# Four gathers of a batch's expert results on GpSimd: one in each of four slots, in place of all four in one slot

## The chip, the cores and the metric

The kernel runs on one core of a Trainium2 chip. Times are device microseconds of one execution of the whole program on that core. The engines are TensorE (PE, with its weight loads as PEld), VectorE (DVE), ScalarE (ACT), GpSimd (POOL) and SyncE (SP, which only issues transfers here).

## The reference, cut to what matters

Eight batches of 256 tokens with 128 features go through a layer norm, and from it through two branches that are added to the input: attention with 16 heads, a linear position bias and two learned null keys, and a mixture of experts (a shared expert, and the two best of eight experts for each token).

```
xn = layernorm(x)
q, k = l2norm(norm(xn) @ Wq) * q_scale, l2norm([null_k, xn @ Wkv_k]) * k_scale
attn = softmax(8 * q @ k.T + slope_h * bias, causal) @ [null_v, xn @ Wkv_v] @ Wout
w = top-2 of sigmoid(xn @ router), normalised
routed = sum over the token's 2 experts e of w_e * (silu(xn @ wg_e) * (xn @ wu_e)) @ wd_e
out = x + attn + shared(xn) + routed
```

## The kernel before, in words

The program has three stages. First the weights are turned and split into a high and a low part, the tokens are routed, and GpSimd scatters each token's row to two places of a DRAM tensor that is sorted by expert (`xg_dram`). Then 39 tiles of 128 rows go through their expert's matrices and are written to `yg_dram`. Last, from about 165 us of the span on, comes the attention stage, with which everything here has to do.

The attention stage works on one batch after the other. Each engine has its own instruction list, written by a function `entry(part, b)`: batch 0 is the part "first", batches 1 to 6 are one loop body "mid", batch 7 is "last", and a short "drain" follows. Each batch has 16 slots `s`, one for each head, and the work on one head is spread over slots by a lag: head `h` has its scores in slot `h` (PE L1072, DVE L885, which adds the bias and finds the maximum), its exponential in slot `h + 1` (ACT L649), its division by the sum in slot `h + 2` (DVE L869), its transposes in slot `h + 3` (PE L1063), and so on. A slot number that a lag drives past 15 falls into the next batch. In a table, `JOBS`, side jobs are laid down slot by slot: the projections of the next batch ("kq", "v"), the transposes of queries and keys ("tr"), the shared expert ("sh") and the final sum of the batch before ("yt"). PE does a side job in its slot, the other engines handle it one slot later. All engines run their lists in order and meet only by semaphores.

GpSimd's list in a batch is this. In slots 0 and 1 it splits the next batch's tokens into a high and a low part (L446, L449; PE's "kq" job of slot 1 waits for the first pair), in slot 2 the same for the current batch (L466, L469). One slot after each "kq" job it raises eight sums of squares to the power -0.5 (`norms`, L415 or L418 and L421; it waits for DVE's L850) and multiplies 512 columns by them (`scale_by_norm`, L431). PE's "kq" jobs stand in slots 1, 4, 5, 6, 7, 11, 12 and 13, so these norms stand in slots 2, 5, 6, 7, 8, 12, 13 and 14. In each odd slot it copies two heads' probabilities of the null keys (L484, `pnull`) after it has waited for DVE's L869 (semaphore `pn`); ACT's L649 may overwrite a ring place of `prob` only after that copy (semaphore `pnc`). In slots 7 and 10 it splits half of the shared expert's hidden values (L457, L459). In slot 10, last, it waits for `fin` (the final sum of the batch before has read `yg` and `w_now`), copies the batch's row numbers and weights (`slot_now` L489, `w_now` L490), waits for these copies, and issues four indirect DMAs (L495) that gather the batch's expert results from `yg_dram` into `yg`: 2 token tiles by 2 experts, 128 rows of 512 bytes each. DVE reads `yg` in the "yt" job, in slot 8 of the next batch (L839).

Of the kernel before, what the change touches and what calls it, by code (L numbers as in the profile page):

```python
# [19 lines left out]
E, I, TOPK = 8, 256, 2  # L20
NT = BATCH * SEQ // P
TB = SEQ // P
# [17 lines left out]
def build(nc, a, out):  # L40


    with ExitStack() as ctx:
        def sb(name, shape, dt=F32):
            return ctx.enter_context(nc.sbuf_tensor(name, shape, dt))
# [8 lines left out]
        yg_dram = nc.dram_tensor("slot_y", [SLOTS, DIM], F32).ap()  # L54
# [34 lines left out]
        def carve(n):  # L89
            at[0] += n  # L90
            return arena_b[:, at[0] - n:at[0]]
# [24 lines left out]
        yg = carve(TB * TOPK * DIM).rearrange("p (t c d) -> p t c d", c=TOPK, d=DIM)  # L116
# [27 lines left out]
        slot_now = sb("slot_now", [P, TB, TOPK], I32)  # L144
# [59 lines left out]
        g = type("Sems", (), S)  # L204
# [48 lines left out]
        def count(part, i, until=HEADS):  # L253

            return sum(1 for job in part_jobs(part, i) if job[0] < until)

        def behind(part, b, s, lag):


            if s < lag:  # L260
                part, b, s = {"mid": "mid", "last": "mid", "drain": "last"}.get(part), b - 1, s + HEADS
            return [(part, b, job) for job in jobs(part, b, s - lag)] if part else []
# [25 lines left out]
        def head_at(part, s, lag):  # L288

            h = s - lag  # L290
            return h if (("own" if h >= 0 else "prev") in PARTS[part]) else None
# [16 lines left out]
        def settled(eng):  # L308


            eng.sem_inc(g.passed, 1)
# [48 lines left out]
        def _(pool):  # L360
# [47 lines left out]
            def norms(b, job):  # L408
                kind, c, w, t, i, n = job
                if kind == "kq":  # L410
                    j = nth(c, w, t)
                    nb = b + 1
                    pool.wait_ge(g.ssm_ready, 8 * nb + j + 1)
                    if w == 0:
                        gp.tensor_tensor(rnorm[:, j, :], ssm[:, j, :], mhalf[:, 0:HEADS // 2],  # L415
                                         ALU.pow).then_inc(g.r_ready, 1)
                    else:
                        gp.tensor_tensor(rpow[:, j, :], ssm[:, j, :], mhalf[:, 0:HEADS // 2],  # L418
                                         ALU.pow).then_inc(g.pw, 1)
                        pool.wait_ge(g.pw, 4 * nb + 2 * c + t + 1)  # L420
                        gp.tensor_tensor(rnorm[:, j, :], rpow[:, j, :], rslope[:, c * 8:c * 8 + 8],  # L421
                                         ALU.mult).then_inc(g.r_ready, 1)

            def scale_by_norm(b, job):
                kind, c, w, t, i, n = job
                if kind == "kq":
                    j = nth(c, w, t)
                    pool.wait_ge(g.r_ready, 8 * (b + 1) + j + 1)
                    pool.wait_ge(left[i], n + 1)
                    rows = (qtok if w else ktok)[t][:, c * 512:(c + 1) * 512].rearrange("p (h d) -> p h d", d=DH)  # L430
                    gp.tensor_tensor(rows, rows, bc(rnorm[:, j, :], DH), ALU.mult).then_inc(g.kqn, 1)  # L431

            def entry(part, b, steps=range(HEADS)):
                whose = PARTS[part]
                nb = b + 1
                for s in steps:
                    if s < 2 and "next" in whose and part != "ready":
                        xT, xs = ((xn2T, xs2), (xn1T, xs1))[s]
                        for _, _, (kind, c, w, t, i, n) in (x for lag in range(1, HEADS) for x in behind(part, b, s, lag)):
                            if (kind, c, w, t) == (("kq", 1, 1, 1), ("v", 0, 0, 1))[s]:  # L440
                                pool.wait_ge(filled[i], n + 1)
                        if part == "first":
                            for i in range(2):
                                pool.wait_ge(filled[i], count("ahead", i) + count("ready", i))
                        settled(pool)
                        gp.tensor_copy(xs[0], xT[:, bass.ds(nb * SEQ, SEQ)]).then_inc(g.xhi, 1)  # L446
                        pool.wait_ge(g.xhi, 2 * nb + s + 1)
                        settled(pool)
                        gp.tensor_tensor(xs[1], xT[:, bass.ds(nb * SEQ, SEQ)], xs[0].bitcast(F32),  # L449
                                         ALU.subtract).then_inc(g.xlo, 1)  # L450
                    if s in (7, 10) and "own" in whose:
                        c = (7, 10).index(s)
                        pool.wait_ge(g.sh_h, 2 * b + c + 1)
                        if part != "first":
                            pool.wait_ge(g.shd, b)
                        settled(pool)
                        gp.tensor_copy(hss[0][:, c * SEQ:(c + 1) * SEQ], hs[:, c, :]).then_inc(g.sh_hi, 1)  # L457
                        pool.wait_ge(g.sh_hi, 2 * b + c + 1)
                        gp.tensor_tensor(hss[1][:, c * SEQ:(c + 1) * SEQ], hs[:, c, :],  # L459
                                         hss[0][:, c * SEQ:(c + 1) * SEQ].bitcast(F32), ALU.subtract).then_inc(g.sh_lo, 1)  # L460
                    if s == 2 and "own" in whose:
                        for _, _, (kind, c, _, t, i, n) in (x for lag in range(1, HEADS) for x in behind(part, b, s, lag)):
                            if (kind, c) == ("sh", 1):
                                pool.wait_ge(filled[i], n + 1)
                        settled(pool)
                        gp.tensor_copy(xs_late[0][:], xn1T[:, bass.ds(b * SEQ, SEQ)]).then_inc(g.late_hi, 1)  # L466
                        pool.wait_ge(g.late_hi, b + 1)
                        settled(pool)
                        gp.tensor_tensor(xs_late[1][:], xn1T[:, bass.ds(b * SEQ, SEQ)], xs_late[0][:].bitcast(F32),  # L469
                                         ALU.subtract).then_inc(g.late_lo, 1)  # L470
                    h = head_at(part, s, 2)
                    for _, job_b, job in (behind(part, b, s, 1) if part != "ahead" else []):
                        norms(job_b, job)
                        scale_by_norm(job_b, job)
                    if h is not None and h % 2:
                        p = h // 2
                        pool.wait_ge(g.pn, TB * (HEADS * b + h + 1))
                        if p == 0 and part != "first":
                            pool.wait_ge(g.pn_hi, 2 * b)
                        settled(pool)  # L480
                        q = p % PAIRS
                        two = prob[:, h % 4 - 1:h % 4 + 1, :]
                        for t, c0 in ((0, 0), (1, K0)):
                            gp.tensor_copy(pnull[:, t, 4 * q:4 * q + 4].rearrange("p (h n) -> p h n", n=2),  # L484
                                           two[:, :, c0:c0 + NNULL]).then_inc(g.pnc, 1)
                    if s == 10 and "own" in whose:
                        pool.wait_ge(g.fin, b + 1)
                        settled(pool)
                        gp.tensor_copy(slot_now[:], slot[:, bass.ds(b * TB, TB), :]).then_inc(g.now, 1)  # L489
                        gp.tensor_copy(w_now[:], wts[:, bass.ds(b * TB, TB), :]).then_inc(g.now, 1)  # L490
                        pool.wait_ge(g.now, 2 * b + 2)
                        settled(pool)
                        for t in range(TB):
                            for c in range(TOPK):
                                pool.indirect_dma_start(yg[:, t, c, :], None, yg_dram,  # L495
                                                        bass.IndirectOffsetOnAxis(ap=slot_now[:, t, c:c + 1], axis=0)
                                                        ).then_inc(g.gath, 16)

            for n in range(NT * TOPK):
                if n == 15:  # L500
                    pool.wait_ge(g.t_ev, 8)
                if n in (15, 22):
                    entry("ahead", -1, [n // 22])
                scatter(n)
# [7 lines left out]
            with pool.Fori(1, BATCH - 1) as b:  # L512
                entry("mid", b)
# [663 lines left out]
```

## Time and profile before

| what | value |
|---|---|
| median of 3 runs | 530.21 us (529.77 to 532.17) |
| the profiled execution | 529.1 us, of which its span 527.4 us |
| mean granted clock of PE in it, share of full speed | 0.96 |
| PE busy, share of the span | 425.0 us, 81% |
| DVE busy | 405.1 us, 77% |
| ACT busy | 358.5 us, 68% |
| POOL busy | 328.2 us, 62% |
| from one batch's first gather to the next one's in the loop | 45.90 us |

The span is the time between the first and the last event that the profiler recorded; 1.7 us of the execution lie around it. Busy times of PE are modelled from its pipelined matmuls, so they are an upper view.

### The profile page before, as it was taken

Reading aid. Unit: us, or ns where it says so; the run is one execution under the profiler, and the core shown is the slowest. Engines: PE = TensorE matmul, PEld = TensorE weight load, DVE = VectorE, ACT = ScalarE, POOL = GpSimd, SP = SyncE. Lnnn points to the kernel's source line nnn. Section 1 sums busy time; section 2 is a strip of 40 time slices with the busy share of each in tenths; the row PEclk is TensorE's granted clock in tenths of the full one; section 3 lists DMA queues with packets and bytes.
Section 4 is the critical chain, followed back from the end, with each engine's and each line's share of the span. In section 5 each row is a group of like instructions: output and inputs, shape, how many; then the busy total and the mean of one; then the engine's idle time right before and its main releaser. Section 6 shows DMA issues by size and latency. Waiting matters only on the chain.

```text
span 527.4 us, 11888 instructions
## 1 busy us (share of the span) xinstructions
PE 425.0 (81%) x2857; PEld 310.8 (59%) x2857; DVE 405.1 (77%) x1466; ACT 358.5 (68%) x1092; POOL 328.2 (62%) x492
## 2 busy tenths in 40 slices
PE   0657243999997889979988996998899699899885
PEld 0555121677775667657656764765676476567663
DVE  3854713666652899888988988998898899889885
ACT  1334123566666878968886895888689688768864
POOL 2275778940002789678867957876795887777140
PEclk9999767899999999989998999999899999989999
DMA  7940111222221000000001000000100000010010
GB/s 219 350 134 32 45 45 59 56 75 79 78 68 32 1 12 11 2 21 22 0 0 30 10 0 20 20 0 0 34 6 0 20 20 0 0 35 5 2 42 10
DMA packets 28159, 21.04 MB, mean 40 GB/s; under 512 B 3512, under 2 KB 25312, under 8 KB 28000
## 3 DMA queue, kind: packets, MB, share of 16 engines
q1 hardware_dynamic: 25264, 16.46, 10.5%
q0 software_dynamic: 2048, 4.20, 2.7%
q8 instruction: 13, 0.21, 0.2%
q14 instruction: 18, 0.15, 0.1%
q10 hardware_dynamic: 816, 0.03, 0.1%
HBM read 12.41 MB, written 8.26 MB: 39 GB/s over the span
## 4 chain that ended last, share of the span: by engine, by line
POOL 31%; PE 21%; issue 20%; DVE 15%; DMA 5%; ACT 4%; POOLq 1%; SPq 1%; DVEq 1%; ACTq 0%
POOL rnorm L415 6%; POOL slot_x L405 6%; POOL arena_b L495 6%; POOL rpow L418 5%; PE bank L1140 4%; PE bank L930 3%; DVE arena_b L885 3%; DVE arena_b L869 3%; POOL pnull L484 3%; PE bank L932 3%; PE bank L931 3%; DMA arena_b<-in_L_ffn_wu_dram 2%; DMA arena_b<-slot_x 2%; PE bank L1072 2%; DVE ssq L846 2%
## 5 line engine op out<-in xcount | busy, mean ns | idle before, releaser
L649 ACT ACTIVATE arena_b<-arena_b,nmx 128x130 f32<-128x130 f32 (+1 forms) x256 | 115.2, 458 | 29.5 <-DVE nmx L885 20.5
L869 DVE TENSOR_SCALAR arena_b<-arena_b,rden 128x130 f32<-128x130 f32 (+1 forms) x256 | 103.9, 450 | 4.5
L885 DVE CUSTOM_DVE_ANT_0 arena_b<-bank,bias 128x130 f32<-128x130 f32 (+1 forms) x256 | 80.9, 353 | 17.1 <-PE bank L1072 9.3
L1072 PE MATMUL bank<-arena_a 64*128 64x130 f32 (+1 forms) x512 | 59.8, 352 | 23.6 <-DVE nmx L885 22.8
L418 POOL TENSOR_TENSOR rpow<-ssm,mhalf 128x8 f32<-128x8 f32 x32 | 52.7, 1648 | 40.4 <-DVE ssm L850 40.4
L1063 PE MATMUL bank<-ident,arena_b 128*128 128x128 f32 x384 | 67.2, 284 | 7.1 <-DVE arena_b L869 7.1
L431 POOL TENSOR_TENSOR arena_b<-arena_b,rnorm 128x512 f32<-128x512 f32 x64 | 67.1, 1048 | 8.4 <-POOL rnorm L421 3.8
L587 ACT ACTIVATE arena_b<-bank 128x512 f32<-128x512 f32 x64 | 38.2, 597 | 31.3 <-PE bank L932 30.5
L415 POOL TENSOR_TENSOR rnorm<-ssm,mhalf 128x8 f32<-128x8 f32 x32 | 52.4, 1639 | 7.7 <-DVE ssm L850 7.7
L846 DVE TENSOR_REDUCE ssq<-arena_b 128x8 f32<-128x512 f32 x64 | 43.4, 678 | 15.5 <-ACT arena_b L587 15.2
L1072 PEld LDWEIGHTS bank<-arena_a 64*128 64x128 f32 x512 | 33.6, 186 | 36.4 <-DVE nmx L885 30.4
L1063 PEld LDWEIGHTS bank<-ident,arena_b 128*128 128x128 f32 x384 | 42.1, 141 | 20.5 <-DVE arena_b L869 12.1
L649 ACT ACTIVATION_READ_ACCUMULATOR arena_b<-arena_b,nmx 128x1 f32 x256 | 50.8, 198 | 0.0
L877 DVE COPY probT<-bank 128x384 f32<-128x384 f32 x64 | 35.5, 555 | 11.1 <-PE bank L1063 7.0
L1053 PE MATMUL bank<-probT,arena_a 128*64 128x256 f32 x256 | 43.1, 410 | 0.8 <-DVE arena_r L860 0.8
L1018 PE MATMUL bank<-ident,arena_b 128*128 128x128 f32 x256 | 39.5, 278 | 4.4 <-ACT arena_a L596 2.8
L405 POOL DMA_INDIRECT slot_x<-arena_a,slot x32 | 32.7, 1022 | 15.6 <-issue 9.2
L495 POOL DMA_INDIRECT arena_b<-slot_y,slot_now x32 | 32.1, 1003 | 13.8 <-issue 7.3
L1018 PEld LDWEIGHTS bank<-ident,arena_b 128*128 128x128 f32 x256 | 29.3, 140 | 16.1 <-issue 9.4
L588 ACT ACTIVATE arena_b<-bank 128x512 f32<-128x512 f32 x64 | 38.1, 596 | 0.0
L446 POOL CAST arena_r<-xn2T 128x256 fp32r (+1 forms) x8 | 3.2, 394 | 54.7 <-PE bank L932 54.7
L484 POOL COPY pnull<-arena_b 128x4 f32<-128x4 f32 x128 | 24.4, 219 | 18.7 <-DVE arena_b L869 18.7
(209 smaller groups left out, 1111.7 us busy)
## 6 DMA issues: line engine op xcount, KB each, us to landing
slot_x<-probT SPq DMA_DIRECT2D x3, 832.0 KB, 9.8
arena_b<-slot_x SPq DMA_DIRECT2D x39, 64.0 KB, 1.9
slot_y<-arena_b SPq DMA_DIRECT2D x39, 64.0 KB, 1.5
arena_b<-in_L_ffn_wd_dram SPq DMA_DIRECT2D x1, 1024.0 KB, 9.4
arena_b<-in_L_attn_Wkv_dram SPq DMA_DIRECT2D x1, 1024.0 KB, 8.6
arena_b<-in_L_attn_x_dram SPq DMA_DIRECT2D x8, 128.0 KB, 2.1
out_dram<-arena_b SPq DMA_DIRECT2D x8, 128.0 KB, 1.8
arena_b<-in_L_attn_Wq_dram SPq DMA_DIRECT2D x1, 512.0 KB, 6.5
```

What stands on the lines that cost most here:

```text
L405: pool.indirect_dma_start(xg_dram, bass.IndirectOffsetOnAxis(ap=slot[:, n // TOPK, n % TOPK:n % TOPK + 1], axis=0), xn1[:, n // TOPK, :], ...
L415: gp.tensor_tensor(rnorm[:, j, :], ssm[:, j, :], mhalf[:, 0:HEADS // 2], ALU.pow).then_inc(g.r_ready, 1)
L418: gp.tensor_tensor(rpow[:, j, :], ssm[:, j, :], mhalf[:, 0:HEADS // 2], ALU.pow).then_inc(g.pw, 1)
L431: gp.tensor_tensor(rows, rows, bc(rnorm[:, j, :], DH), ALU.mult).then_inc(g.kqn, 1)
L495: pool.indirect_dma_start(yg[:, t, c, :], None, yg_dram, bass.IndirectOffsetOnAxis(ap=slot_now[:, t, c:c + 1], axis=0)).then_inc(g.gath, 16)
L649: sc.activation(prob[:, h % 4, c], sim[h % 2][:, c], ACT.Exp, scale=-1.0, bias=nmx[:, h % HEADS, t:t + 1], accum_out=den[:, h % HEADS, t:t ...
L846: ve.reduce_sum(ssq[j % 2][:], sqb[j % 2].rearrange("p (h d) -> p h d", d=DH), AX.X).then_inc(g.red, 1)
L869: ve.tensor_scalar(pr, pr, rden[:, h % HEADS, t:t + 1], None, ALU.mult).then_inc(g.pn, 1)
L885: ve.tensor_tensor_reduce(out=sim[h % 2][:, c], in0=bank[h % 2][:, c], in1=bias[:, c], scale=-SLOPES[h], scalar=3e38, op0=ALU.add, op1=ALU ...
L1018: ins = te.transpose(side[i][:, q * P:(q + 1) * P], src[:, p * P:(p + 1) * P], ident[:])
L1063: ins = te.transpose(bank[2 + h % 2][:, k * P:(k + 1) * P], prob[:, h % 4, c:c + P], ident[:])
L1072: ins = te.matmul(bank[half][:, c0:c1], qT[r, h // 2, q0:q0 + P], kT[r, h // 2, 0:c1 - c0], start=True, stop=True)
```

## The change

The condition around the four issues is moved. In place of all four in slot 10, behind the copy of the row numbers, gather 0 stays in slot 10, and gathers 1, 2 and 3 come last in GpSimd's slots 11, 12 and 13. Their order, their operands and what they signal are the same, and no wait is added or taken away.

```
                         gp.tensor_copy(w_now[:], wts[:, bass.ds(b * TB, TB), :]).then_inc(g.now, 1)
                         pool.wait_ge(g.now, 2 * b + 2)
                         settled(pool)
-                        for t in range(TB):
-                            for c in range(TOPK):
-                                pool.indirect_dma_start(yg[:, t, c, :], None, yg_dram,
-                                                        bass.IndirectOffsetOnAxis(ap=slot_now[:, t, c:c + 1], axis=0)
-                                                        ).then_inc(g.gath, 16)
+                    if 10 <= s < 10 + TB * TOPK and "own" in whose:
+                        t, c = (s - 10) // TOPK, (s - 10) % TOPK
+                        pool.indirect_dma_start(yg[:, t, c, :], None, yg_dram,
+                                                bass.IndirectOffsetOnAxis(ap=slot_now[:, t, c:c + 1], axis=0)
+                                                ).then_inc(g.gath, 16)
```

## Rows read from the trace of the kernel before

**Rows 1.** The page's busy time: engine, us, share of the span.

```profile
PE 425.0 (81%) x2857; PEld 310.8 (59%) x2857; DVE 405.1 (77%) x1466; ACT 358.5 (68%) x1092; POOL 328.2 (62%) x492
```

**Rows 2.** Waits in 215 to 495 us: us in total, times, longest.

```profile
POOL rpow L418 <- DVE ssm L850: 36.4, 18, 3.4
...
ACT arena_b L649 <- POOL pnull L484: 5.3, 6, 0.9
...
PEld bank L930 <- POOL arena_r L449: 3.6, 5, 0.7
...
PE bank L930 <- POOL arena_r L449: 2.4, 5, 0.5
```

**Rows 3.** Busy time of the engines from 376 to 398 us.

```profile
376.00:398.00 22.00, 21.52 (x168) 15.67 (x164) 20.15 (x77) 19.11 (x60) 18.13 (x29) 1.00 0.05 12
```

**Rows 4.** POOL in order of time, a batch of the loop: start, us.

```profile
371.97 1.64 POOL L418 TENSOR_TENSOR rpow<-ssm,mhalf 128x8 f32<-128x8 f32 x1 [1.58 <-DVE ssm L850]
...
377.68 1.08 POOL L495 DMA_INDIRECT arena_b<-slot_y,slot_now  x1 [0.80 <-POOL w_now L490]
379.06 0.95 POOL L495 DMA_INDIRECT arena_b<-slot_y,slot_now  x1 [0.30 <-issue]
380.32 1.05 POOL L495 DMA_INDIRECT arena_b<-slot_y,slot_now  x1 [0.30 <-issue]
381.68 0.94 POOL L495 DMA_INDIRECT arena_b<-slot_y,slot_now  x1 [0.30 <-issue]
382.63 0.42 POOL L484 COPY pnull<-arena_b 128x4 f32<-128x4 f32 x2
383.02 1.67 POOL L418 TENSOR_TENSOR rpow<-ssm,mhalf 128x8 f32<-128x8 f32 x1
...
392.41 0.39 POOL L446 CAST arena_r<-xn2T 128x256 fp32r x1
392.99 0.72 POOL L449 TENSOR_TENSOR arena_r<-xn2T,arena_r 128x256 fp32r<-128x256 f32 x1 [0.19 <-POOL arena_r L446]
```

**Rows 5.** DVE in order of time, the same batch.

```profile
371.72 0.17 DVE L850 TENSOR_SCALAR ssm<-ssq 128x8 f32<-128x8 f32 x1
...
377.50 0.55 DVE L869 TENSOR_SCALAR arena_b<-arena_b,rden 128x130 f32<-128x130 f32 x2
...
380.00 0.56 DVE L869 TENSOR_SCALAR arena_b<-arena_b,rden 128x130 f32<-128x130 f32 x2
...
381.28 0.17 DVE L850 TENSOR_SCALAR ssm<-ssq 128x8 f32<-128x8 f32 x1
...
385.40 1.12 DVE L869 TENSOR_SCALAR arena_b<-arena_b,rden 128x130 f32<-128x130 f32 x2
...
391.22 1.20 DVE L869 TENSOR_SCALAR arena_b<-arena_b,rden 128x130 f32<-128x130 f32 x2
```

**Rows 6.** PE in order of time, the next batch's slots 1 to 3.

```profile
393.77 0.50 PE L930 MATMUL bank<-wq_hi,arena_r 128*128 128x512 f32 x1 [0.48 <-POOL arena_r L449]
...
400.84 0.93 PE L1072 MATMUL bank<-arena_a 64*128 64x130 f32 x8 [0.35 <-DVE nmx L885]
```

**Rows 7.** POOL in order of time: a scatter behind a tensor instruction.

```profile
65.72 1.00 POOL L405 DMA_INDIRECT slot_x<-arena_a,slot  x1 [0.16 <-issue]
```

**Rows 8.** POOL, then DVE, in batch 0: the same places.

```profile
199.42 1.67 POOL L418 TENSOR_TENSOR rpow<-ssm,mhalf 128x8 f32<-128x8 f32 x1
...
197.44 0.17 DVE L850 TENSOR_SCALAR ssm<-ssq 128x8 f32<-128x8 f32 x1
```

**Rows 9.** ACT, the exponential of slot 13 in batch 7.

```profile
512.11 0.41 ACT L649 ACTIVATE arena_b<-arena_b,nmx 128x130 f32<-128x130 f32 x1 [1.72 <-POOL pnull L484]
```

**Rows 10.** The line L495: from issue to landing.

```profile
DMA to landing us min/median/max: 2.4/2.6/3.5
```

## The prediction

> **What bounds the kernel now.** I first read the page's busy times [rows 1]. No engine is full, so the shares alone decide nothing: PE has 81%, DVE 77%, POOL 62%. In the attention stage a batch takes 45.90 us, and the four gathers stand where three engines are dense together: from 376 to 398 us PE is busy for 21.5 of 22 us, DVE for 20.2 and POOL for 18.1 [rows 3]. Next the waits of the loop [rows 2]. POOL waits 36.4 us in total for DVE's L850, but always in the first half of a batch; in the second half others wait for POOL: PE's "kq" matmul of slot 1 for the split L449 (PEld up to 0.7 us, five times), and ACT's exponential for the copy L484 (0.9 us, six times). So POOL's list from slot 10 to slot 0 of the next batch is on the path that sets a batch's length, and it is enough to follow it in order of time [rows 4]. After the fourth gather POOL doesn't wait once for another engine until slot 0: it is behind, and works off its list. From the end of gather 0 at 378.76 to the first split of the next batch at 392.41 it takes 13.65 us. The split L449 then ends at 393.71 and PE starts on it at 393.77, after 0.48 us of idle [rows 6].
>
> **What the change removes, adds and moves.** No instruction is added or removed. On POOL, gathers 1, 2 and 3 move behind the copy L484 of slot 11, behind the norms of slot 12, and behind norms and copy of slot 13. What is still behind the last of them is slot 14's norms, slot 15's copy, and slot 0.
>
> Slot 11: the copy needs head 9's L869, which ends at 378.05 [rows 5], before gather 0 ends at 378.76. So it runs at once (0.42 us) and stands 3.87 us earlier than now. Gather 1 follows. The price of a gather after a tensor instruction isn't shown, but a scatter behind one is: 0.16 us of gap and 1.00 us [rows 7]. So gather 1 ends at 378.76 + 0.42 + 1.16 = 380.34.
>
> Slot 12: here a wait appears. The power L418 needs DVE's L850, which ends at 381.28 + 0.17 = 381.45 [rows 5]. In slot 8 the power started 0.08 us after that instruction's end (371.89 to 371.97) [rows 4, 5]. So it starts at 381.53, and POOL has been idle for 1.2 us, where now it isn't idle at all. DVE can't be earlier: nothing of the change reaches it before then, and PE and DVE are both nearly full there [rows 3]. The power starts 383.02 - 381.53 = 1.49 us earlier than now.
>
> Slots 12 to 15: the norms and copies take what they take now (9.39 us from 383.02 to 392.41), and gathers 2 and 3 come on top, 2 x 1.16 = 2.32 us. Both later sums of squares are ready in time, since POOL reaches them at most 0.4 us earlier than now, or later. So slot 0 begins 2.32 - 1.49 = 0.83 us later than now. In batch 0 the same sum is 199.42 - (197.44 + 0.17 + 0.08) = 1.73 us gained [rows 8], and 2.32 - 1.73 = 0.59 us lost. The gain that one might expect, that the norms come sooner, is real only for slots 11 and 12, and nobody waits for these.
>
> Both ends of the gather's price: with no gap and the shortest duration it is 0.94 us, and the shift 1.88 - 1.49 = 0.39 us. With the gap of the first gather now (0.80 us, of which part is a wait for its row numbers) and 1.08 us, it is 1.88, and the shift 3.76 - 1.49 = 2.27 us. I take 1.16, since rows 7 is the one row with a tensor instruction in front. The gaps of 0.30 between gathers now are behind another gather [rows 4].
>
> How much of 0.83 us reaches the end of the batch: PE starts the "kq" of slot 1 0.83 us later, and does the rest of slots 1 to 3 behind it. But in slot 3 it waits 0.35 us for DVE in any case [rows 6], so only what exceeds 0.35 goes on: 0.48 us a batch. Behind that point the stage is a chain of waits between PE, ACT and DVE, and I know of no cover. Slot 0's splits stand in batches 1 to 6 only. So the loss is 0.24 (behind batch 0) + 5 x 0.48 = 2.6 us.
>
> The end gains: batch 7 has no splits in slot 0 and no norms in slots 12 to 14, so there only the copies count. Behind batch 6, ACT's wait of 0.9 us [rows 2] shrinks, because the copy of slot 13 comes 1.49 - 1.16 = 0.33 us earlier: -0.3 us. In batch 7 ACT waits 1.72 us for the copy behind four gathers [rows 9]; this copy now stands behind one. DVE's scores are ready about 0.8 us before 512.11, so no more than that can be won, and I take 0.5 us, since DVE has further waits behind it.
>
> Sum: 2.6 - 0.3 - 0.5 = +1.8 us. The landing is no term: a gather lands 2.6 us after its issue [rows 10], and DVE reads `yg` only in slot 8 of the next batch, in batch 7 at the very end, after more than 10 us. The other side of POOL's order is free too: `fin` is waited for as before, ahead of gather 0.
>
> **A rule on the shared port.** Now gathers that start during DVE's L869 (377.68 and 380.32) take 1.08 and 1.05 us, the others 0.95 [rows 4, 5]: 0.1 us more. The Trainium skill ("SBUF — State Buffer", Who interferes with whom, and the warning on descriptors in SBUF: two separate sides) says that a DVE instruction in a two-port mode holds the port pair that it shares with GpSimd for its whole length, so that GpSimd can't write descriptors. By this rule gather 2, which will stand across slot 14's L869, would be held for all of it. By the trace it is 0.1 us.
>
> **The rivals.**
> 1. *The whole shift goes through* (slower): PE's 0.35 us is no cover, for example because ACT's line behind the "kq" (its square, two copies, the exponential) is itself without a gap. Then the loss is 0.59 + 5 x 0.83 = 4.7 us, less 0.8: +3.9 us, 534.1. For it speaks that ACT has its own work behind that matmul.
> 2. *DVE sets the pace and becomes faster* (faster). DVE's L869 takes 0.55 us beside a gather or a power, and 1.12 and 1.20 us in slots 14 and 0, where it runs beside L431 [rows 4, 5]. With the new order a gather stands beside slot 14's and a power beside slot 0's, which gives up to 0.57 + 0.65 = 1.2 us a batch. It decides only if slot 0 on POOL isn't later than now, that is if the gathers cost no more than 0.75 us each there. Then PE could win its idle of 0.48 us [rows 6] in six batches, 2.9 us, and the end 0.8: -3.7 us, 526.5. Against it: no gather in the trace takes less than 0.94.
> 3. *A gather is held by DVE* for a whole L869 (0.55 us in place of 0.1), one gather a batch: 6 x 0.45 = 2.7 us on top of the sum, 534.7. Against it stand the 1.05 to 1.08 us of now. This is what the page's rule would make of it.
> 4. *Each separate gather pays the first one's gap*: shift 2.27 us, in batch 0 3.76 - 1.73 = 2.03, so 5 x 1.92 + 1.68 - 0.8 = +10.5 us, 540.7.
>
> **How the numbers follow.** By its own time the profiled execution goes from 529.1 to 530.9 us (span 527.4 to 529.2). The median before is 530.21, 1.1 above the profiled execution, and I put the 1.8 us on it: 532.0. Chances: this forecast 0.45, rival 1 0.25, rival 2 0.1, rival 3 0.08, rival 4 0.05, something else 0.07. The range reaches from the lower end of the gather's price, 529.6 (no loss behind batch 0 to 5, and the end's gain), rounded out a little to 529.0, up to 535.5, past rivals 1 and 3; rivals 2 and 4 are left out. A measurement can tell about 0.5%, 2.65 us, from no change, that is 527.6 to 532.9. Of the forecast's 0.45, 0.38 lies inside this; rivals 1, 3 and 4 lie above it, rival 2 below it but for a part. That makes faster 0.1, same 0.48, slower 0.42.
>
> **What would show it right or wrong.** In POOL's line of the changed kernel: L484 of slot 11 directly behind gather 0; a wait of 1.0 to 1.3 us for DVE's L850 before slot 12's L418, seven times, where there is none now; gathers with gaps near 0.16 us; L446 of slot 0 some 14.5 us after the end of gather 0 in place of 13.65. PE's wait for L449 grows from 0.5 to about 1.3 us; ACT's waits for L484 shrink, the one of 1.72 us is gone. The distance of two batches' first gathers goes from 45.90 to about 46.4 us. L869 in slots 14 and 0 is back at 0.55 us. The prediction is wrong if DVE delivers slot 12's sum sooner than now (then POOL doesn't wait), if a separate gather costs clearly more or less than 1.16 us, or if slots 1 to 3 swallow all or nothing of the shift.

## The result and the profile after

The changed kernel takes **538.14 us** (median of six runs, 536.07 to 542.12), the kernel before beside it 529.99 us (six runs, 528.74 to 532.17). The ratio is 1.0166, with a 95% interval of 1.0118 to 1.0214: slower by 8.2 us. Forecast were 532.0 us and a range of 529.0 to 535.5. The sign of the sum was right, its size was not. The profiled execution is the slowest of the six, 542.12 us with a span of 540.4 us, so the spans of the two profiles differ by 13.0 us, more than the medians do.

The waits between 215 and 495 us of the changed kernel, in the order of [rows 2] (us in total, times, longest):

```profile
POOL rpow L418 <- DVE ssm L850: 44.2, 20, 4.8
...
PEld bank L930 <- POOL arena_r L449: 9.8, 5, 2.0
PE bank L930 <- POOL arena_r L449: 8.6, 5, 1.8
...
ACT arena_b L649 <- POOL pnull L484: 6.1, 6, 1.1
```

GpSimd's list over one batch of the loop and into the next, the lines that answer to [rows 4]:

```profile
338.26 1.07 POOL L495 DMA_INDIRECT arena_b<-slot_y,slot_now  x1 [0.80 <-POOL w_now L490]
339.35 0.32 POOL L484 COPY pnull<-arena_b 128x4 f32<-128x4 f32 x2
339.82 0.97 POOL L495 DMA_INDIRECT arena_b<-slot_y,slot_now  x1 [0.15 <-issue]
342.11 1.68 POOL L418 TENSOR_TENSOR rpow<-ssm,mhalf 128x8 f32<-128x8 f32 x1 [1.32 <-DVE ssm L850]
...
344.22 1.04 POOL L431 TENSOR_TENSOR arena_b<-arena_b,rnorm 128x512 f32<-128x512 f32 x1 [0.16 <-POOL rnorm L421]
345.43 1.05 POOL L495 DMA_INDIRECT arena_b<-slot_y,slot_now  x1 [0.16 <-issue]
346.51 1.68 POOL L415 TENSOR_TENSOR rnorm<-ssm,mhalf 128x8 f32<-128x8 f32 x1
...
349.87 1.06 POOL L495 DMA_INDIRECT arena_b<-slot_y,slot_now  x1 [0.16 <-issue]
...
354.18 0.39 POOL L446 CAST arena_r<-xn2T 128x256 fp32r x1
```

The reader is to see four things. The copy of slot 11 stands directly behind gather 0. Slot 12's power waits 1.32 us for DVE's sum, where it waited for nothing. It starts 2.78 us after the end of gather 0 (339.33 to 342.11); the forecast had 2.77. And from the end of gather 0 to the first split L446 it is now 14.85 us, where it was 13.65 and 14.5 were forecast. Up to the power the forecast holds to 0.01 us, so the rest lies behind it, in the two gathers there. From the start of slot 12's power to the first split it was 9.39 us (383.02 to 392.41), and it is now 12.07 us (342.11 to 354.18) with two gathers in it. So a separate gather costs 2.68 / 2 = 1.34 us of the list and not 1.16. Its 0.16 us of gap is right. But it takes 1.05 us and not 1.00 (the median of the 32 is 1.052 us, and before it was 0.952), and 0.13 us more go where it meets the next instruction. The kernel before shows the same place without a gather:

```profile
385.13 1.04 POOL L431 TENSOR_TENSOR arena_b<-arena_b,rnorm 128x512 f32<-128x512 f32 x1 [0.16 <-POOL rnorm L421]
386.13 1.64 POOL L415 TENSOR_TENSOR rnorm<-ssm,mhalf 128x8 f32<-128x8 f32 x1
```

There the power starts 0.04 us before the recorded end of L431 and takes 1.64 us. Behind a gather it starts 0.03 us after the gather's end and takes 1.68.

PE, in two neighbouring batches, from the wait for L449 on (to be laid beside [rows 6]):

```profile
355.54 0.56 PE L930 MATMUL bank<-wq_hi,arena_r 128*128 128x512 f32 x1 [1.70 <-POOL arena_r L449]
355.89 0.63 PE L931 MATMUL bank<-wq_hi,arena_r 128*128 128x512 f32 x1
356.32 0.63 PE L932 MATMUL bank<-wq_lo,arena_r 128*128 128x512 f32 x1
356.74 1.06 PE L1018 MATMUL bank<-ident,arena_b 128*128 128x128 f32 x4
...
404.12 0.50 PE L930 MATMUL bank<-wq_hi,arena_r 128*128 128x512 f32 x1 [1.69 <-POOL arena_r L449]
404.45 0.39 PE L931 MATMUL bank<-wq_hi,arena_r 128*128 128x512 f32 x1
404.68 0.39 PE L932 MATMUL bank<-wq_lo,arena_r 128*128 128x512 f32 x1
404.91 0.60 PE L1018 MATMUL bank<-ident,arena_b 128*128 128x128 f32 x4
```

The wait has grown from 0.48 to 1.7 us, as much as the shift of 1.20 us. What the prediction had not reckoned with stands behind it: in the one batch the same instructions take 0.63 and 1.06 us, in the other 0.39 and 0.60. The windows around the first of them (busy us of PE, PEld, DVE, ACT and POOL, then the granted clock of PE) give the reason:

```profile
353.00:355.00 2.00, 0.84 (x9) 0.43 (x5) 1.97 (x7) 0.95 (x4) 1.81 (x5) 1.00 0.00 0
355.00:357.00 2.00, 1.46 (x5) 1.11 (x6) 1.53 (x6) 0.61 (x3) 1.81 (x5) 0.71 0.00 0
357.00:359.00 2.00, 2.00 (x10) 1.68 (x8) 0.95 (x3) 1.58 (x3) 1.43 (x4) 0.50 0.00 0
359.00:361.00 2.00, 2.00 (x17) 1.42 (x18) 0.72 (x5) 1.86 (x7) 1.76 (x3) 0.93 0.00 0
```

Behind the wait the granted clock falls from 1.00 (2.4 GHz) to 0.50 (1.2 GHz). The shares missing in the three windows add up to 0.58 + 1.00 + 0.14 = 1.7 us of full clock, just where PE already is late. It happens in three of the loop's six batches: behind the waits that end at 260, 356 and 451 us, and not behind two equally long ones in between. The Trainium skill ("TensorE: Matmul & The Clock Gate", Part 1: The HAM clock gate) says that TensorE is granted 1.2 GHz or 2.4 GHz, by how busy it has lately been; the two levels are these, and a fall behind an idle stretch is what the rows show.

How the 13.0 us lie over the span, by the start of the copy to `w_now` in each batch (worked out from the timelines of both profiles):

| stretch | before, us | after, us | difference |
|---|---|---|---|
| start to batch 0 | 193.18 | 193.97 | +0.8 |
| batch 0 to 1 | 45.72 | 47.67 | +1.95 |
| batch 1 to 6, no fall in slot 1 (two) | 45.88, 45.89 | 46.68, 46.68 | +0.8 each |
| batch 1 to 6, fall in slot 1 (three) | 45.89, 45.89, 45.89 | 48.82, 48.57, 48.29 | +2.9, +2.7, +2.4 |
| batch 6 to 7 | 37.51 | 38.53 | +1.0 |
| batch 7 to the end | 21.50 | 21.17 | -0.3 |

So the shift costs 0.8 us an interval, and a fall of the clock in slot 1 about 2 us more (5.6 us over the three). The kernel before has such falls too, four of 1.7 us of full clock in its loop, but all of them 38 to 39 us behind the copy to `w_now`, in the middle of the next batch. The interval of 45.89 us that holds one at 369 us is as long as the ones without. What counts is where the clock falls.

Not all of the 13.0 us come from the change. In the profile of the changed kernel the clock also falls ahead of batch 0's gathers, where the two kernels' lists are still the same. The same window, before and then after:

```profile
190.00:192.00 2.00, 1.24 (x13) 1.00 (x13) 1.77 (x8) 1.26 (x5) 1.84 (x6) 1.00 0.02 4
```

```profile
190.00:192.00 2.00, 2.00 (x13) 1.41 (x11) 1.08 (x4) 1.32 (x5) 1.84 (x3) 0.50 0.00 0
```

Behind it DVE's sum for slot 12 comes late, and so does the rest of the batch. Eleven of the study's fourteen profiles have such a fall between 186 and 197 us, the kernel before on the second chip among them, and in all eleven this sum starts 5.6 to 6.3 us behind the copy to `w_now`. In the three without it (the kernel before here, and the two runs below that move gathers into the next batch's slot 3) it is 4.3 us. The first experiment below has this fall, but in its loop a list no longer than before, and its interval from batch 0 to 1 is 46.61 us: some 0.9 us of the 1.95 go with the fall.

### The profile page after: what moved, and what is told of

Read it like the earlier page. It is cut to its first block, busy times and chain, and to the rows that moved or that the text cites. A ratio compares the mean times of both kernels' runs of the same rounds, so it can differ in the third digit from the quotient of the medians.

```text
span 540.4 us, 11888 instructions
## 1 busy us (share of the span) xinstructions
PE 433.5 (80%) x2857; PEld 317.5 (59%) x2857; DVE 402.3 (74%) x1466; ACT 360.4 (67%) x1092; POOL 331.7 (61%) x492
## 4 chain that ended last, share of the span: by engine, by line
PE 30%; POOL 24%; issue 19%; DVE 14%; DMA 5%; ACT 5%; SPq 1%; POOLq 1%; DVEq 1%; ACTq 0%
POOL slot_x L405 6%; POOL rnorm L415 5%; PE bank L930 4%; POOL arena_b L495 4%; PE bank L932 4%; PE bank L931 3%; POOL rpow L418 3%; PE bank L1072 3%; PE bank L1140 3%; DVE arena_b L885 3%; DVE arena_b L869 3%; DMA arena_b<-slot_x 3%; PE bank L1063 2%; PE bank L1053 2%; POOL pnull L484 2%
## 5 line engine op out<-in xcount | busy, mean ns | idle before, releaser
L869 DVE TENSOR_SCALAR arena_b<-arena_b,rden 128x130 f32<-128x130 f32 (+1 forms) x256 | 97.3, 429 | 4.6
L1072 PE MATMUL bank<-arena_a 64*128 64x130 f32 (+1 forms) x512 | 62.8, 366 | 22.8 <-DVE nmx L885 22.0
L1063 PE MATMUL bank<-ident,arena_b 128*128 128x128 f32 x384 | 68.6, 289 | 6.4 <-DVE arena_b L869 6.4
L431 POOL TENSOR_TENSOR arena_b<-arena_b,rnorm 128x512 f32<-128x512 f32 x64 | 67.1, 1049 | 8.4 <-POOL rnorm L421 3.8
L1072 PEld LDWEIGHTS bank<-arena_a 64*128 64x128 f32 x512 | 35.6, 196 | 35.8 <-DVE nmx L885 29.3
L1063 PEld LDWEIGHTS bank<-ident,arena_b 128*128 128x128 f32 x384 | 43.2, 144 | 19.8 <-DVE arena_b L869 11.3
L877 DVE COPY probT<-bank 128x384 f32<-128x384 f32 x64 | 35.6, 556 | 13.2 <-PE bank L1063 9.5
L1018 PE MATMUL bank<-ident,arena_b 128*128 128x128 f32 x256 | 40.9, 285 | 3.7 <-ACT arena_a L596 2.2
L495 POOL DMA_INDIRECT arena_b<-slot_y,slot_now x32 | 33.1, 1033 | 11.3 <-POOL w_now L490 6.5
L1018 PEld LDWEIGHTS bank<-ident,arena_b 128*128 128x128 f32 x256 | 30.4, 144 | 15.9 <-issue 8.3
L446 POOL CAST arena_r<-xn2T 128x256 fp32r (+1 forms) x8 | 3.2, 395 | 55.9 <-PE bank L932 55.9
L484 POOL COPY pnull<-arena_b 128x4 f32<-128x4 f32 x128 | 24.6, 221 | 20.0 <-DVE arena_b L869 19.8
```

The costliest lines, as they stand in the source:

```text
L495: pool.indirect_dma_start(yg[:, t, c, :], None, yg_dram, bass.IndirectOffsetOnAxis(ap=slot_now[:, t, c:c + 1], axis=0)).then_inc(g.gath, 16)
L869: ve.tensor_scalar(pr, pr, rden[:, h % HEADS, t:t + 1], None, ALU.mult).then_inc(g.pn, 1)
L1018: ins = te.transpose(side[i][:, q * P:(q + 1) * P], src[:, p * P:(p + 1) * P], ident[:])
L1063: ins = te.transpose(bank[2 + h % 2][:, k * P:(k + 1) * P], prob[:, h % 4, c:c + P], ident[:])
L1072: ins = te.matmul(bank[half][:, c0:c1], qT[r, h // 2, q0:q0 + P], kT[r, h // 2, 0:c1 - c0], start=True, stop=True)
```

## The experiments

All ratios are to runs of the kernel before on the same chip. Two chips were used: on the first the kernel before took 530.03 us (median of 23), on the second 536.49 (17) and 536.07 (22). Where an experiment has added lines, the later line numbers are 1 to 3 higher (L498 is L495).

**The idle filled.** If the loss is the idle before slot 12's power and gathers behind it, then gathers that fill the idle must take it back.

```diff
-                    if 10 <= s < 10 + TB * TOPK and "own" in whose:
-                        t, c = (s - 10) // TOPK, (s - 10) % TOPK
+                    for n in ({10: (0,), 11: (1, 2), 13: (3,)}.get(s, ()) if "own" in whose else ()):
+                        t, c = n // TOPK, n % TOPK
```

> Gather 0 in slot 10, gathers 1 and 2 in slot 11, gather 3 in slot 13: the changed kernel with gather 2 one slot earlier. Theory A (GpSimd idles 1.31 us before slot 12's power, and the two gathers behind it push slot 0 later): gather 2 costs 1.29 us on GpSimd's line and fills that idle time, so slot 0's L446 comes 13.5 to 13.7 us after the end of gather 0, as before (13.65; changed kernel 14.85), PE waits about 0.5 us for L449 and not 1.7, and the time is that of the kernel before, 529 to 531 us. Rival B (each gather that stands alone costs something by itself, by its gap or by VectorE's port): two of the three lone places are left, and at least half of the loss stays, 534 us or more.

It took 529.75 us (527.06 to 530.64), ratio 0.9979 (0.9960 to 0.9999). GpSimd's list in order of time:

```profile
379.92 0.32 POOL L484 COPY pnull<-arena_b 128x4 f32<-128x4 f32 x2
380.40 0.97 POOL L495 DMA_INDIRECT arena_b<-slot_y,slot_now  x1 [0.15 <-issue]
381.67 0.94 POOL L495 DMA_INDIRECT arena_b<-slot_y,slot_now  x1 [0.30 <-issue]
382.70 1.67 POOL L418 TENSOR_TENSOR rpow<-ssm,mhalf 128x8 f32<-128x8 f32 x1
```

Only 0.08 us of idle are left before the power, the loop's intervals are 45.66 to 45.69 us, and PE waits 0.27 us. That refutes rival B of the expectation, which kept at least half of the loss. The second form has the dictionary `{10: (0,), 11: (1, 2, 3)}`, all three in slot 11:

> Gather 0 in slot 10, gathers 1, 2 and 3 in slot 11, behind the copy L484. Theory A: only the copy comes forward by 3.9 us; nothing idles before slot 12's power, slot 0 is where it was, and in batch 7 ScalarE's wait of 1.7 us goes: 529 to 530.5 us. Rival B: no loss either, since the gathers stand together. Rival D (the copy's earlier place is what harms): slower than before by more than 3 us.

529.04 us (527.85 to 530.67), ratio 0.9986 (0.9971 to 1.0001), intervals of 45.66 us, a wait of 0.25. The earlier copy does no harm, so rival D is refuted too. Both take the whole loss back, and in the first a gather by itself in slot 13 does no harm, since another one has filled the idle ahead of slot 12's power.

**The gathers where GpSimd has time.** If GpSimd's list from slot 10 to slot 0 sets the length of a batch, it must be worth something to take gathers out of it. Here a batch's gathers stand in slots 3 and 4 of the next batch, and batch 7's in its own slot 10.

```diff
+                    here = {10: (0, 1, 2, 3)} if part == "last" else {}
+                    if part in ("mid", "last"):
+                        here = {3: (0, 1), 4: (2, 3), **here}
+                    for n in here.get(s, ()):
+                        t, c = n // TOPK, n % TOPK
```

> Batches 0 to 6: the four gathers leave slots 10 to 13 and stand in slots 3 and 4 of the next batch, two in each, where GpSimd waits 3.4 us for VectorE's sum of slot 5; batch 7 has all four in slot 10. Theory A: GpSimd's list from slot 10 to slot 0 is about 5 us shorter, L449 is ready before PE asks for it, and PE's wait (0.5 us before the change, 1.7 after) is 0 in batches 1 to 6: 3 us faster than before, 526 to 528 us. It waits instead for VectorE's sums in slots 12 to 14. If the four gathers (5.2 us) overrun the 3.4 us of idle time and slot 5's power gets onto the path, the gain is lost: 530 us or more. Rival B expects no gain from an earlier L449: 530 us.

It took **522.82 us** (519.18 to 526.88), ratio 0.9872 (0.9833 to 0.9912), the first kernel of the study that is faster than before. Intervals are 44.26 us. GpSimd, in two places of a batch:

```profile
332.92 1.64 POOL L418 TENSOR_TENSOR rpow<-ssm,mhalf 128x8 f32<-128x8 f32 x1 [2.98 <-DVE ssm L853]
...
342.03 0.40 POOL L446 CAST arena_r<-xn2T 128x256 fp32r x1
...
351.49 1.08 POOL L498 DMA_INDIRECT arena_b<-slot_y,slot_now  x1 [0.16 <-issue]
352.87 0.95 POOL L498 DMA_INDIRECT arena_b<-slot_y,slot_now  x1 [0.30 <-issue]
354.13 0.94 POOL L498 DMA_INDIRECT arena_b<-slot_y,slot_now  x1 [0.30 <-issue]
355.38 0.94 POOL L498 DMA_INDIRECT arena_b<-slot_y,slot_now  x1 [0.30 <-issue]
356.35 1.68 POOL L418 TENSOR_TENSOR rpow<-ssm,mhalf 128x8 f32<-128x8 f32 x1
```

In slot 12 it now waits 2.98 us for DVE, so of the 4.9 us of gathers that left only 1.8 shorten the list (14.07 us from the copy to `w_now` to the split, before 15.84), and the batch by 1.6. PE waits for no split any more. The gain is larger than the 3 us expected, which counted PE's wait alone: five intervals are 1.6 us shorter each, and the one behind batch 0 by 1.8. In the chain that ended last the shares have turned over, first the kernel before, then this one:

```profile
POOL 31%; PE 21%; issue 20%; DVE 15%; DMA 5%; ACT 4%; POOLq 1%; SPq 1%; DVEq 1%; ACTq 0%
```

```profile
PE 47%; DVE 21%; issue 11%; POOL 7%; ACT 6%; DMA 5%; SPq 1%; DVEq 1%; ACTq 0%; POOLq 0%
```

On the second chip the same was tried by halves: gathers 0 and 1 in the own slot 11, 2 and 3 in slot 3 of the next batch (batch 7: slots 11, 12 and 13).

> Gathers 0 and 1 in slot 11, where GpSimd now waits 3.0 us for slot 12's sum, gathers 2 and 3 in slot 3 of the next batch, where it waits 3 us for slot 5's; batch 7 has them in slots 11, 11, 12 and 13. With all four in slots 3 and 4 (522.8 us) slot 5's power came 1.8 us late. Theory A: each pair (2.5 us) fits into idle time, nothing on GpSimd is late, and the time is that of the late gathers or up to 2 us below, 520 to 523.5 us. If pairs cost time by their number of places, it is between them and before: 525 us.

525.66 us (524.84 to 526.79), ratio 0.9820 (0.9794 to 0.9847), intervals of 44.78 us. The expected 520 to 523.5 us were missed. The ratio is better than the 0.9872 of all four moved, but the kernel before is 6 us slower on this chip. By the intervals, moving all four is the better order: 44.26 against 44.78 us.

**The clock alone.** If the falls in slot 1 cost time of their own, then the changed kernel must win when PE is kept busy during its wait. Ten useless matmuls of 128 columns (the profile shows each as two) go ahead of the "kq" matmul of slot 1 in batches 1 to 6; nothing else differs from the changed kernel.

```diff
+                if (kind, c, w, t) == ("kq", 0, 1, 0) and not isinstance(n, int):
+                    for k in range(10):
+                        te.matmul(side[i][:, 0:P], ident[:], ident[:], start=True, stop=True)
```

> The changed kernel, and in batches 1 to 6 PE does ten more matmuls of 128 columns on the identity into the side bank that its slot-1 job is going to overwrite, just before it waits for L449: work without use, about 1.4 us, inside the wait of 1.7 us. Theory C (a part of the loss is that PE's granted clock falls to 1.2 GHz behind this wait in four of six batches, which costs about 2 us each time): the granted clock stays at 1.00 in slot 1, all distances of first gathers are about 46.7 us, and the time is 533.5 to 536 us, 2 to 5 us below the changed kernel. If the clock there costs nothing, the time stays at 538 us or rises.

537.93 us (535.56 to 539.07, five runs), ratio 1.0141 (1.0117 to 1.0165). PE and the windows at the place shown above:

```profile
352.98 2.40 PE L1011 MATMUL bank<-ident 128*128 128x128 f32 x20
355.13 0.48 PE L930 MATMUL bank<-wq_hi,arena_r 128*128 128x512 f32 x1
355.45 0.39 PE L931 MATMUL bank<-wq_hi,arena_r 128*128 128x512 f32 x1
```

```profile
353.00:355.00 2.00, 2.00 (x21) 2.00 (x20) 1.57 (x8) 1.26 (x5) 1.81 (x6) 1.00 0.00 0
355.00:357.00 2.00, 2.00 (x17) 1.78 (x15) 1.53 (x5) 0.79 (x2) 1.63 (x6) 1.00 0.00 0
```

The falls in slot 1 are gone (the expectation speaks of four, the changed kernel's profile has three) and the loop's intervals are even, 46.96 to 46.98 us. But ten matmuls last 0.3 us longer than the wait. The profile's span is 4.0 us below that of the changed kernel, but the median doesn't stand apart from its 538.14 us, and the expected 533.5 to 536 us were missed. So it was repeated on the second chip with eight (`range(8)`), beside the changed kernel once more.

> The changed kernel as it is, once more, beside the other runs of this call: 535 to 540 us, a ratio of 1.010 to 1.020. Its distances of first gathers are either about 46.7 us, where the granted clock stays up in slot 1, or 48 to 49 us, where it falls.

540.05 us (538.84 to 541.48), ratio 1.0087 (1.0057 to 1.0117), below the 1.010 to 1.020 expected: the kernel before lost more on this chip than the changed one. Its intervals are 46.68 to 46.79 us without a fall in slot 1 and 48.30 and 48.56 with one.

> As the run with ten matmuls without use in PE's wait of slot 1 (2.15 us, 0.3 us longer than the wait), now with eight (1.72 us), which fit into it. Theory C (the fall of the clock behind the wait costs about 2 us each time): no fall in slot 1, all distances in the loop 46.6 to 46.8 us, and the time 1 to 4 us below the changed kernel of the same call. If the clock costs nothing, the two are the same.

536.36 us (533.50 to 542.32, twelve runs), ratio 1.0003 (0.9975 to 1.0032). Both were run once more in the last series:

> The changed kernel once more, beside the others of this call: 1.008 to 1.018 of the kernel before; some distances of first gathers at 46.7 us, those with a fall of the granted clock in slot 1 at 48 to 49 us.

540.30 us (537.49 to 543.37), ratio 1.0089 (1.0061 to 1.0117). Three intervals with a fall in slot 1 take 48.25 to 48.34 us. In all, the three profiles of the changed kernel have eighteen waits of 1.4 to 1.8 us there, and eight of them are followed by a fall.

> The changed kernel with eight matmuls without use in PE's wait of slot 1, once more. Theory C: 2 to 5 us below the changed kernel of this call, as in the last call (536.4 against 540.1 us), and no fall of the clock in slot 1.

536.54 us (533.89 to 539.05, twelve runs), ratio 1.0022 (1.0002 to 1.0042). PE in one place of its loop, and the window behind it:

```profile
350.28 1.95 PE L1011 MATMUL bank<-ident 128*128 128x128 f32 x16
352.14 0.50 PE L930 MATMUL bank<-wq_hi,arena_r 128*128 128x512 f32 x1
```

```profile
352.00:354.00 2.00, 2.00 (x16) 1.71 (x14) 1.56 (x5) 0.97 (x3) 1.81 (x6) 1.00 0.00 0
```

There is no fall in slot 1. Four of its five intervals from batch 1 to 6 are 46.65 to 46.78 us; the fifth, 47.28, holds a fall twice as long as the others right ahead of a copy to `w_now`. Useless work on PE makes the changed kernel faster by 3.7 and by 3.8 us, with GpSimd's list as it was.

**The delay alone.** Is a later slot 0 enough, or does something in the separate gathers do harm? Here the kernel before, with its four gathers in slot 10, gets a useless instruction on GpSimd in slot 14 of batches 0 to 6. First an add of 512 columns and a copy of 4:

> The kernel before, with its four gathers together in slot 10, and two instructions without use on GpSimd at the start of slot 14's work in batches 0 to 6 (512 columns added, 4 copied), about 1.2 us: the size of the shift that the change made. Theory A (only the later slot 0 counts, however it comes about): PE's wait for L449 grows from 0.5 to 1.7 us, the distance of first gathers goes to 46.7 us or more, the clock falls in slot 1 in some batches, and the time is 534 to 540 us, as with the change. Rival B (lone gathers harm by themselves): no more than 1 or 2 us slower than before.

543.36 us (541.64 to 545.07), ratio 1.0141 (1.0108 to 1.0174), above the 534 to 540 us expected. This was more than a delay, as the order of time of both engines shows:

```profile
400.61 1.27 POOL L476 TENSOR_TENSOR ed<-ed 128x512 f32<-128x512 f32 x1
400.70 1.53 DVE L872 TENSOR_SCALAR arena_b<-arena_b,rden 128x130 f32<-128x130 f32 x2
```

DVE's division takes 1.53 us beside the add. Beside the gather of 338.26 in the changed kernel, and beside powers, it takes 0.55. So the run doesn't tell the theories apart. The second form has no wide operand:

```diff
+                    if s == 14 and part in ("first", "mid"):
+                        gp.tensor_tensor(spare[:, 0:6], ssm[:, 7, 0:6], mhalf[:, 0:6], ALU.pow)
```

> The kernel before, with one power of six columns without use on GpSimd behind slot 14's norms in batches 0 to 6, about 1.2 us; the first delay of this kind used a 512-column addition, which ran beside VectorE's divisions and stretched them (L869 1.5 us). VectorE's divisions ran at 0.55 us beside powers. Theory A (only a later slot 0 counts): PE's wait for L449 is about 1.7 us, the distances 46.7 us and more, the ratio to before that of the changed kernel in this call or up to 0.002 above. Rival B (lone gathers harm by themselves): at most 1.003.

539.60 us (536.63 to 541.43), ratio 1.0083 (1.0053 to 1.0113), against 1.0089 for the changed kernel. The power lasts 1.32 us. That is the ratio expected if only a later slot 0 counts; rival B allowed at most 1.003. From the copy to `w_now` to the split it is 16.96 to 17.13 us in batches 2 to 5 (changed kernel 17.04), and their intervals are 46.70 to 46.77 (changed kernel without a fall 46.68). A delay of GpSimd's list costs time without any separate gather. But the expected wait of 1.7 us isn't there: PE waits only 0.3 to 0.5 us, because something else has held it up (last section), and in slot 1 the clock doesn't fall. So the time of this run isn't the changed kernel's by the same sum, and the equal ratios are in part chance. What a delay by itself costs in the loop is read from the kernel before on this chip (next run): two of its intervals are 46.11 and 46.12 us, so it is 0.6 us. Its other three, 46.84 to 47.83 us, hold a fall of twice the usual length or come right behind one, and can't be compared.

**The kernel before, against itself:**

> The kernel before against itself: a ratio of 1.000. Its runs had a median of 530.0 us in one call and of 536.5 us in the next. If the chip of this call is again a slow one, the distances of first gathers (45.9 us in the first profile) show where the time is: with falls of the granted clock in slot 1, or with longer slots elsewhere.

535.73 us (533.70 to 540.59, twelve runs), ratio 1.0000 (0.9975 to 1.0026).

## Why the prediction was wrong, point by point

- *POOL's list from slot 10 to slot 0 sets a batch's length*: right. A longer list gives longer intervals (46.7 with the useless power), a shorter one shorter (44.26, 44.78). The same reading could have said more: that gathers taken out of this list are worth time.
- *An idle before slot 12's power, 1.2 us*: right, 1.32 us, and the power started within 0.01 us of the forecast. In slot 11 the copy and gather 1 came as worked out.
- *A separate gather costs 1.16 us*: too little, 1.34. The row of the scatter [rows 7] has its gap right, not its duration, and the slower start and run of the power behind a gather has no term. With two gathers behind the power that made the shift 2 x 1.34 - 1.48 = 1.20 us in place of 0.83. Rivals 3 and 4 are refuted: gaps of separate gathers in the loop are 0.15 and 0.16 us (0.39 once), and no gather of the changed kernel took more than 1.09 us. Gather 0 began at 338.26 during a division of 0.55 us (338.09 on) and took 1.07 us.
- *A gather that starts during a division takes 0.1 us more*: this reading doesn't hold in the kernel before itself. In batch 7 the gather with no division at its start is the long one, and the one that starts during a division is short:

```profile
506.85 1.08 POOL L495 DMA_INDIRECT arena_b<-slot_y,slot_now  x1 [0.81 <-POOL w_now L490]
508.23 0.95 POOL L495 DMA_INDIRECT arena_b<-slot_y,slot_now  x1 [0.30 <-issue]
```

```profile
507.71 0.55 DVE L869 TENSOR_SCALAR arena_b<-arena_b,rden 128x130 f32<-128x130 f32 x2
```

What makes some gathers 0.1 us longer is open. The Trainium skill's rule on the shared port ("SBUF — State Buffer", Who interferes with whom) would hold a gather for the rest of a division in a two-port mode, 0.5 us by the prediction's rival 3; no gather here shows that, and which mode the division runs in the profile doesn't tell. The Trainium skill's rule in that section that the second of the two engines blocks until the first is done fits the division that takes 1.53 us beside the wide add: it ends 0.35 us behind the add, and its second half takes 0.35 us.
- *0.35 us of the shift are swallowed in slot 3*: right. In the changed kernel's intervals without a fall PE no longer waits for DVE there (the place of [rows 6]):

```profile
410.77 0.93 PE L1072 MATMUL bank<-arena_a 64*128 64x130 f32 x8
```

Of 1.20 us, 0.8 reach the interval. With the right price of a gather the step would have given 1.20 - 0.35 = 0.85.
- *Batch 0, 0.24 us*: wrong, 1.95. The prediction took DVE's sum there at the place of before. It came 4.79 us after the start of gather 0 (195.00 to 199.79), and not 3.41 (194.20 to 197.61), so the power gained 0.3 us and not 1.73. DVE is later in every profile in which the clock has fallen ahead of these gathers, with the change and without it. About 1 us is left for the change, still some four times the forecast.
- *Behind batch 6, -0.3 us*: wrong, 1.0. In the two other profiles of the changed kernel this interval is 37.90 and 37.89 us, 0.4 above before. In this profile the clock is low from 472 to 479 us, twice as long as in the other falls, DVE's next sum comes 0.6 us late, and the interval is 0.6 us longer than in those two.
- *ACT's waits for L484 shrink*: not in total, 5.3 to 6.1 us. The wait for slot 13's copy is gone in five of the loop's six batches, more than forecast, but a new one of 1.05 us stands at slot 15's copy, which the longer list has made late.
- *The end, -0.5 us*: about right. ACT's wait of 1.72 us is gone, and the stretch behind batch 7's copy is shorter by 0.3.
- *PE waits 1.3 us in place of 0.5*: 1.7. **The step that failed** was what stands behind this wait. The sum carried it as so much idle time, let PE go on at full speed, and has no term for the clock at all. The granted clock falls behind about every second such wait, and the fall isn't hidden there: it costs about 2 us each, 5.6 us in the profiled execution. The runs with eight matmuls show it: 3.7 and 3.8 us less for the same list on GpSimd.
- *Rival 2, DVE becomes faster*: its divisions did (slot 14's takes 0.66 us and slot 0's 0.55, where they took 1.12 and 1.20 [rows 5]), and it won nothing, since slot 0 came later all the same.
- *The lower end of the range*: a small slip. With no loss in the loop and the end's gain the sum gives 529.4, not 529.6. It decided nothing.

By the profile the 13.0 us are 5 x 0.8 for the shift, 5.6 for the clock in slot 1, 1.95 behind batch 0, 1.0 behind batch 6, 0.8 ahead of batch 0's copy, and -0.3 at the end. The 0.8 and some 0.9 of the 1.95 stem from a place where the lists are still the same, and 0.6 of the 1.0 go with a long fall of the clock that nothing here ties to the change. What is left is 10.7 us, in the slowest of six executions; the medians differ by 8.2.

## What to carry to other kernels

A wait of PE isn't priced by its length alone: look in the windows at what the granted clock does behind such idle stretches, and whether PE is late at that place. Before work is spread out on an engine, ask for each new place whether the engine idles just ahead of it; work that is moved from before a wait to behind it isn't hidden, it is added. And where an engine's list is found to set the length of a loop, look first for a stretch in which the same engine waits: the same four gathers, moved there, made the kernel 1.3% faster. And before a difference of two profiles is put down to a change, look for falls of the clock at places that the change can't have reached.

## What was unexpected in the hardware

The two chips differ by 6 us for the kernel before, and the profiles show a part of it. On the second chip the kernels with the four gathers together in slot 10 have one more idle stretch of DVE in each batch of the loop, right before slot 12's scores; the releaser isn't one that the profile can name. The kernel before, the order of time of DVE:

```profile
388.17 0.17 DVE L850 TENSOR_SCALAR ssm<-ssq 128x8 f32<-128x8 f32 x1
390.53 0.29 DVE L885 CUSTOM_DVE_ANT_0 arena_b<-bank,bias 128x130 f32<-128x130 f32 x1 [2.19 <-remote]
```

In this profile, the slowest of its twelve executions, it adds up to 11.2 us in six waits of up to 2.2 us, and ACT has seven more of up to 1.6 us. In the two runs with a delay on that chip it is 13.2 and 12.1 us in six. The changed kernel, the one with eight matmuls and the one with two gathers moved have no such wait of DVE on the same chip, nor has any profile on the first. The waits aren't lost time one for one: two intervals with such a stall are 46.11 and 46.12 us, 0.2 above the first chip's, and most of the difference lies in the intervals with a longer fall of the clock or one ahead of them, and behind batch 7's copy (24.47 us, where it was 21.50). The change costs 1.7% on one chip and 0.9% on the other; that it takes away a stall of the kernel before on the second would fit, but isn't shown. What stalls DVE is open. That it goes with four gathers close together in slot 10 is what these profiles have in common, and no more; no run was made for it.
